# Attention, layernorm and int8 feed-forward on eight cores: the attention group's output copy moved from VectorE to ScalarE

## The reference

```python
q1, k1, q2, k2, v = (heads(x @ w.T) for w in (q1_w, k1_w, q2_w, k2_w, v_w))
attn1 = softmax(q1 @ k1^T / sqrt(128));  attn2 = softmax(q2 @ k2^T / sqrt(128))
out = (attn1 - lam * attn2) @ v                     # per head, then heads joined
x = layernorm(x + out @ o_w.T)
q, in_scale = per_token_quant_int8(x)               # round(x / scale), scale = absmax / 127
f = (q @ weight.T) * in_scale * w_scale + bias      # as float16
x = layernorm(x + f)
```

## Time and profile before

| | |
|---|---|
| median of 2 runs | 3657.73 us (3656.45 to 3659.0) |
| profiled execution, device time | 3655.73 us |
| its span on the slowest core (core 3) | 3654.2 us |
| spans of all 8 cores | 3646.6 to 3654.2 us |
| mean granted TensorE clock, all cores | 0.940 to 0.942 of full speed |
| PE busy | 3121.9 us (85%) |
| DVE busy | 1357.4 us (37%) |
| ACT busy | 1266.2 us (35%) |

### The profile page before, as it was taken

The page is one execution under the profiler, slowest core; times in us unless marked ns, Lnnn a source line. Parts: engine busy times, 40 slices in busy tenths (PEclk is TensorE's granted clock), DMA queues, the critical chain, the costliest instruction groups (busy, mean ns, idle before and its releaser), DMA issues. The chain is left out here.

```text
span 3654.2 us, 45468 instructions; the slowest of 8 cores (3646.6 to 3654.2 us)
## 1 busy us (share of the span) xinstructions
PE 3121.9 (85%) x16640; PEld 1412.3 (39%) x16640; DVE 1357.4 (37%) x1585; ACT 1266.2 (35%) x1459; POOL 19.1 (1%) x40
## 2 busy tenths in 40 slices
PE   1999999999989899989899999999998276664897
PEld 1443434343435353534444343434343033222343
DVE  0143333333232424342433333342334144444377
ACT  0252433434251616151524333342515122222432
POOL 0000000000000000000000000000000000000000
PEclk9999999999999999999999999999999687776799
DMA  9101010101010101101010101010000532222233
GB/s 146 33 5 31 5 32 4 32 4 34 3 34 2 34 9 29 28 8 31 5 31 5 32 4 32 4 32 4 5 3 5 99 102 75 79 70 69 92 109 117
DMA packets 89494, 135.07 MB, mean 37 GB/s; under 512 B 72640, under 2 KB 72640, under 8 KB 82880
## 3 DMA queue, kind: packets, MB, share of 16 engines
q0 software_dynamic: 6672, 58.72, 9.2%
q1 hardware_dynamic: 82608, 73.43, 6.7%
HBM read 157.29 MB, written 33.55 MB: 52 GB/s over the span
## 5 line engine op out<-in xcount | busy, mean ns | idle before, releaser
L259 ACT ACTIVATE pb<-psA 128x1024 bf16<-128x1024 f32 x512 | 524.4, 1024 | 1480.0 <-PE psA L224 1480.0
L241 PE MATMUL pS<-pb,ones 128*128 128x512 bf16 x2048 | 623.9, 387 | 0.0
L259 ACT ACTIVATE pb<-psB 128x1024 bf16<-128x1024 f32 x512 | 524.1, 1024 | 172.3 <-PE psB L224 172.3
L237 PE MATMUL pO<-pb,vv 128*128 128x512 bf16 x1024 | 394.9, 386 | 148.8 <-DVE sc_ L43 96.8
L206 PE MATMUL psA<-xTb,wq 128*128 128x512 bf16 x2048 | 463.0, 379 | 0.0
L206 PE MATMUL psB<-xTb,wq 128*128 128x512 bf16 x2048 | 462.9, 379 | 0.0
L43 DVE RECIPROCAL r<-sc_ 128x512 f32<-128x512 f32 x128 | 429.1, 3353 | 13.2
L43 DVE COPY oc<-pO 128x1024 f32<-128x1024 f32 x64 | 78.4, 1225 | 909.6 <-PE pS L241 909.6
L237 PE MATMUL pO<-pb,v 128*128 128x512 bf16 x1024 | 394.7, 385 | 0.0
L224 PE MATMUL psA<-q,k 128*128 128x512 bf16 x1024 | 314.6, 390 | 18.2 <-DVE k L43 18.2
L224 PE MATMUL psB<-q,k 128*128 128x512 bf16 x1024 | 312.5, 388 | 0.0
(11 more groups left out here) (72 smaller groups left out, 1962.6 us busy)
## 6 DMA issues: line engine op xcount, KB each, us to landing
wq<-wqkv POOLq DMA_DIRECT2D x16, 2560.0 KB, 18.3
xin<-x SPq DMA_DIRECT2D x16, 1024.0 KB, 5.7
out<-oo SPq DMA_DIRECT2D x16, 1024.0 KB, 4.8
xTb<-xT POOLq DMA_DIRECT2D x1, 8192.0 KB, 57.0
osc<-oout SPq DMA_DIRECT2D x256, 32.0 KB, 1.5
woS<-wo POOLq DMA_DIRECT2D x16, 512.0 KB, 13.0
ocol<-osc SPq DMA_DIRECT2D x64, 128.0 KB, 2.6
ysc<-yf SPq DMA_DIRECT2D x16, 512.0 KB, 3.0
```

What stands on the lines that cost most here:

```text
L237: te.matmul(pO[:, j * 512:(j + 1) * 512], vv[:, cc * 128:(cc + 1) * 128], pslc, start=(cc == 0), stop=(cc == NC_ - 1))
L241: mm = te.matmul(pS[:, j * 512:(j + 1) * 512], ones_sb[:], pslc, start=(cc == 0), stop=(cc == NC_ - 1))
L259: sc.activation(pb_sb[:, (c % 2) * 1024:(c % 2) * 1024 + 1024], sbank[c % 2][:], AF.Exp, scale=INV_SQRT_HD,).then_inc(sEXP, 1)
```

## The change

The copy of `pO` moves from DVE to ACT, behind the 16 exps of its group. It counts a new semaphore, `sOC2`; `sOC` now counts only the copy of `pS`. PE's PV 0 waits for both, each up to `grp`. ACT's copy waits for the last PV of its group, and from the third group on for the division of two groups before (`sCB`), which read the same half of `oc_sb`. DVE's `divide` waits for ACT's copy of its group. The functions are otherwise unchanged.

```diff
@@ attention, tensor, pv_issue
                             if cc == 0 and grp > 0:
-                                te.wait_ge(sOC, 2 * grp)
+                                te.wait_ge(sOC, grp)
+                                te.wait_ge(sOC2, grp)
@@ attention, scalar, after the 16 exps of a group
                         ).then_inc(sEXP, 1)
+                    sc.wait_ge(sPVD, NC_ * (grp + 1))
+                    if grp >= 2:
+                        sc.wait_ge(sCB, grp - 1)
+                    sc.copy(oc_sb[:, (grp % 2) * 1024:(grp % 2) * 1024 + 1024],
+                            pO[:]).then_inc(sOC2, 1)
@@ attention, vector
                 def divide(g2):
                     b2 = (g2 % 2) * 1024
+                    ve.wait_ge(sOC2, g2 + 1)
                     if g2 >= 2:
                         ve.wait_ge(sODMA, 64 * (g2 - 1))
...
                         ve.wait_ge(sPVD, NC_ * (grp + 1))
                         b = (grp % 2) * 1024
-                        ve.tensor_copy(oc_sb[:, b:b + 1024], pO[:], inc=(sOC, 1, 2 * grp + 1))
-                        ve.tensor_copy(sc_sb[:, b:b + 1024], pS[:], inc=(sOC, 1, 2 * grp + 2))
+                        ve.tensor_copy(sc_sb[:, b:b + 1024], pS[:], inc=(sOC, 1, grp + 1))
@@ second block, tensor
                     te.wait_ge(sCB, H * QT)
-                    te.wait_ge(sOC, 2 * H * QT)
+                    te.wait_ge(sOC, H * QT)
+                    te.wait_ge(sOC2, H * QT)
```

More of the change, by code:

```diff
@@ L96, in build_program @@
          sVST, sSQT, sWF, sWC, sYI, sZ2, sPF, sOUTV, sOUT, sVS2, sSQ2, sID, sVC, sOC,
-         sST, sYR, sAFF, sS2T, sAF2, sWO2, sWO3, sWO4, sTQ2, sTQ3) = [
+         sST, sYR, sAFF, sS2T, sAF2, sWO2, sWO3, sWO4, sTQ2, sTQ3, sOC2) = [
             E(nc.semaphore(n)) for n in (
@@ L102, in build_program @@
                 "sYI", "sZ2", "sPF", "sOUTV", "sOUT", "sVS2", "sSQ2", "sID", "sVC", "sOC",
-                "sST", "sYR", "sAFF", "sS2T", "sAF2", "sWO2", "sWO3", "sWO4", "sTQ2", "sTQ3")]
+                "sST", "sYR", "sAFF", "sS2T", "sAF2", "sWO2", "sWO3", "sWO4", "sTQ2", "sTQ3", "sOC2")]
         with nc.Block() as blk0:
```

## The result

The changed kernel takes 3583.3 us in the median of all its runs; the comparison, which leaves out the executions in which one die shows a lower granted clock than the other, gives a ratio of 0.9798 to the kernel before, with a 95% interval of 0.9779 to 0.9817. That is 2.0% faster, some 74 us. The forecast was 3558 us, so the direction and most of the size came out, and 25 us did not.

The account below looks back on a forecast made before the run. TensorE, busy 85% of the span, was the bound: time could be won only in its idle stretches or low clock. 30.2 + 20.0 + 1.3 + 48.3 = 99.8 us off 3655.7, plus 2.0 for the median: 3558 us, range 3544 to 3585.

Parts of the forecast that it names:

- Part 1 and 3: DVE's queue moves up 1.33 us; at a head's end the third projection starts that much earlier, 15 x 1.33 = 20.0 us.
- Parts 2 and 6: Inside a head, PV 0 starts 0.63 us earlier, released by exp 0: 48 x 0.63 = 30.2 us; new waits cost nothing.
- part 6: The new waits on DVE (sOC2) and ACT (sCB, sPVD) add nothing beyond exp 0's delay, already costed.
- Part 5: At inner boundaries PE's idle stretch falls from 2.01 to 1.38 us, so 27 clock falls go away: 48.3 us.
- Part 4: After the last group, the last division starts 1.33 us earlier, and the barrier and output projection's loads follow: 1.3 us.
- a slow copy: ACT's pO copy at a group's end taking DVE's 1.225 us without any overlap: 14.6 us less gain.
- falls that stay: A quarter of the clock falls at inner boundaries staying: 12 us, counted in the range's upper end.
- A: Rival: the clock still falls at inner boundaries, only 51.5 us won, 3606 us; in whole or mostly, 9%.
- B: Rival: ACT's copy at each boundary forces two table loads, exp 0 2.57 us later, 3767 us, slower; 4%.
- C: Rival: the two PSUM copies at a boundary hinder each other, both stretching to 1.5 us, 3634 us; 3%.

Follow-up runs that it names:

- experiment 1: The changed kernel with PE's PV 0 waiting for the two copies first and for the exp last: 3569.6 us, ratio 0.9757.
- experiments 2 and 3: Changed kernel plus two or four satisfied PE waits: 3605.0, 3662.6 us; ScalarE copying pO only at head ends: 3633.9; kernel before with earlier VectorE pO copy: 3596.5 us.

## Why the prediction was right, and where 25 us went

**Part 1 and 3, DVE's queue and a head's end: right.** 15 waits took 0.18 us each (0.15 forecast). Head intervals went from 96.08 to 94.85 us where nothing fell: 1.23 instead of 1.33. The missing 0.1 us is the third wait in PE's queue, ahead of the first PV of a head, whose copies are long done (PE's stretch there grew from 0.99 to 1.10 us); this extra wait was in the change, and part 6 of the prediction cost only ACT's and DVE's new waits, not PE's.

**Parts 2 and 6, inside a head: right mechanism, one term mis-sized.** The ACT copy (1.012 us for 1.02), the spacing (0.91 for 0.92), and exp 0 as what is late next were right. The step that failed is "PE starts PV 0 at 404.86 + 0.15". The 0.15 us were read where one wait stands ahead of the products, and were carried to a place with two more waits behind it. Those cost 0.105 us each, so the term is 48 x 0.44 = 21.1 us and not 30.2. With the waits in the other order (experiment 1) the stretch is 1.37 us, against 1.38 forecast. The Trainium skill, page Perfetto Trace Analysis, section Identifying Dependency Chains, says that an instruction that waits on several engines may have separate semaphore instructions put in front of it. The profile doesn't show such instructions, but the times agree with it: each further wait took 0.105 us of PE's queue.

**Part 5, the clock: right in what came, but its argument did not reach so far.** None of the 48 inner boundaries falls in the changed kernel. The prediction's reason was that 1.38 us is shorter than the 1.48 us that never fell. The stretch came out at 1.58 us, longer than that, so the reason given didn't cover it, and that the falls went away all the same was in part luck. Only the experiments show that there was room: no inner boundary fell behind 1.79 us. Two things were mis-sized. The price of a fall was read from one interval, 26.41 - 24.62 = 1.79 us; the 27 intervals of core 3 with a fall took 1.50 to 1.97 us more than 24.62, 46.4 us together, which is 1.9 less than the 48.3 of the sum. And new falls came at head starts: three on the profiled core, 5.5 us together, and three or four on the others. The prediction looked for falls only where they were; the idle pair at a head's start had been there before too (1.12 and 0.99 us) without one fall in 15.

**Part 4, the end: not seen.** The stages after attention took 5.6 us more instead of 1.3 less. On the eight cores they take 802.0 to 806.0 us before and 801.7 to 807.7 after: the difference is within what cores differ by, and the slowest core was one with a long end. The prediction had put 10 us on this, as an estimate; which moment of the end makes it long wasn't tested.

Together, for the attention stage of the two profiled cores: 98.5 forecast (30.2 + 20.0 + 48.3), 78.5 measured. The waits inside heads cost 9.1 (30.2 - 21.1), those at head starts 1.5 (20.0 - 15 x 1.23), the new falls 5.5, the price of a fall 1.9, and longer intervals without a fall 1.9, most of it in 12 inner intervals of 24.46 us instead of 24.18 (six of that kind before). With the end's 5.6 + 1.3 = 6.9 us and the start's 0.4 this is the gap of 27.3 us between 99.8 and 72.5. In the mean of the eight cores the gap lies almost wholly in the attention stage: 73.8 us of 98.5, in part because the mean core had 24.9 falls and not the 27 of core 3.

What makes an interval 0.28 us longer stays open, but the trace has a trail. Each of the 12 on core 7 has an exp that starts late, and 0.6 to 0.7 us behind its start a packet of the DMA queue q14, of kind instruction, starts; the same holds for the six on core 3 before (0.6 to 0.9 us). One of them, from the timeline, and q14 in the 2 us from 890:

```profile
887.23 1.02 ACT L260 ACTIVATE pb<-psA 128x1024 bf16<-128x1024 f32 x1 [0.46 <-PE psA L224]
...
890.30 1.02 ACT L260 ACTIVATE pb<-psA 128x1024 bf16<-128x1024 f32 x1 [0.75 <-PE psA L224]
...
q14 instruction: 1, 0.01, 1.3%
```

The stage has some 50 such packets, and most fall where nothing is late. No run tests whether they have to do with it.

**The range.** 3583.3 us lies in the stated range of 3544 to 3585 us, 1.7 us from its upper end. That it lies inside is in part luck: the upper end was made of a slow copy (14.6 us) and of falls that stay (12 us). Neither came; the waits and the falls at new places took about their room.

**The rivals.** A (the clock still falls at inner boundaries) did not happen; experiments 2 and 3 show from where on it would have. B (table loads) did not: one load at L260. C (the two copies hinder each other) did not: 1012 and 1225 ns, with `pS` as fast as before.

## What to carry to other kernels

Ahead of an instruction on PE with several waits, put the wait that ends last at the end, and count every wait that a change adds to PE's queue, satisfied ones too; look at ScalarE's queue in the same way. When PE's idle stretches are near a length behind which its clock has fallen, a few tenths of a microsecond less in each can be worth several times their own length; look at the granted clock around each kind of boundary, of both the falls that are there and the idle stretches that have none yet. Before work is moved to another engine, see whether it could start earlier where it is.

## What the runs showed of the hardware

- A satisfied semaphore wait in PE's queue, behind the one that ended last, took 0.105 us: the stretch was 1.37, 1.58, 1.79 and 2.00 us with zero, two, four and six of them. In ACT's queue one such wait took 0.055 us (the copy's idle time 1.31 instead of 1.26 us).
- TensorE's granted clock went from 2.4 to 1.2 GHz behind a single idle stretch of 2.0 us at 16 to 29 of a core's 48 inner boundaries, in three kernels, and behind one of 0.93 to 1.94 us at none.
- It also fell behind a pair of stretches, 1.12 us and 0.89 to 1.52 us with 1.02 us of work between them, at none to 15 of 15 head starts, depending on the kernel, the core and the execution. For this alone the same program had attention stages 24.7 us apart between its cores, and 0.5 us apart when the pair was shortened to one stretch of 0.69 us.
- A ScalarE copy of 128x1024 f32 from PSUM into SBUF took 1.012 us beside a VectorE copy of 1.225 us from other PSUM banks, which took 1.225 us before as well. No run has the ScalarE copy without the other beside it.
